# Storing the high part of the experts' gate and up weights by itself, ahead of the low part's subtraction

## The chip, the cores and the metric

The kernel runs on one core of a Trainium2 chip. The metric is the device time of one execution in microseconds (us); lower is better. The numbers of before are the median of 3 runs and one profiled execution.

## What is computed

Two pre-norm layers on 2048 tokens of 512 features, all in float32. The part that matters here is the first attention and the weights that are prepared beside it:

```python
x = x + _L0_attn_ref(_layernorm(x), Wq, bq, Wk, bk, Wv, bv, Wo, bo)   # 2 sequences of 1024 tokens, 16 heads of 32
x = x + _L0_ffn_ref(_layernorm(x), gate_w, w_gate_proj, w_up_proj, w_down_proj)   # 32 experts, 8 of them for each token
x = x + _L1_attn_ref(_layernorm(x), w_in, w_param, w_out)             # state-space layer
x = x + _L1_ffn_ref(_layernorm(x), lut, gate_idx, up_idx, down_idx)   # weights from a 16-entry table

# _L0_ffn_ref, what an expert e computes
g = jnp.einsum('th,eih->tei', x, w_gate_proj)     # i = 192 columns
u = jnp.einsum('th,eih->tei', x, w_up_proj)
h = jax.nn.silu(g) * u * masked_w[:, :, None]
out = jnp.einsum('tei,ehi->th', h, w_down_proj)
```

## The kernel before

The kernel is written by hand, engine by engine. Each stage is a block in which every engine has its own instruction list and semaphores order them; the next block begins when all engines have ended this one. The stages are: layernorm and q, k, v projection; attention (`attend`); output projection; mixture of experts; state-space layer; table feed-forward.

Products in float32 precision are made as sums of three products of a rounded "high" part (type fp32r) and the "low" rest. The experts' weights are split into those two parts before the mixture of experts needs them, on GpSimd (POOL), beside the attention, and are stored in a DRAM tensor `w_split`, from which the mixture of experts reads them for every block of tokens.

In `attend` there are 16 heads, two to a loop body, the first and the last body written out and six turns of a loop between them. POOL's list for one head, in the order of the code, is:

- `take_v` (L577): it copies the head's values into `v_pair`, one of two buffers, which TensorE (PE) needs for the head's outputs (L752, `ps_y<-probs,v_pair`). TensorE waits on `v_ready` for it, `take_v` waits until the head before the last has been used up.
- twice (for two experts) `split_gate_up` (L581 to L596): a cast of `e_raw_gu` (128 partitions x 1536 elements, 6 KB each) into the first half of `e_gu_parts` (L588), a subtraction into the second half (L591), one transfer of both halves to `w_split`, 12 KB of each partition (L594), and the load of the expert after next into `e_raw_gu` (L567). Ahead of the cast it waits for the load, and for the store of the head before out of the same of two buffers (`gu_stored`).
- after each of them `split_down` (L598 to L619): two casts (L607, L608), two subtractions (L611, L614), the store of `e_dn_parts` (L617), of which there is one buffer, and the next load (L570). Ahead of L607 it waits until the store of the expert before has landed (`dn_stored`).

After the 32 experts POOL splits the output projection's weights (L637, L640) and ends its list with waits for all stores. All transfers issued by POOL use queue q0, those issued by SyncE (SP) use q1. SP loads the next heads' q and k (L651, L655) and stores the head's output rows out of `y_st` (L667, L668), for which DVE's copy L860 of the next head waits. The next block, `output_projection`, begins with the load `o_sums<-prob_sums` (L925).

Of the kernel before, what the change touches and what calls it, by code (L numbers as in the profile page):

```python
# [6 lines left out]
F32 = mybir.dt.float32  # L7
# [19 lines left out]
HEADS = 16  # L27
# [463 lines left out]
def attend(nc, qk, v_rows, yT, all_sums, w_raw, w_split, wo, wo_hi, wo_lo):  # L491
# [18 lines left out]
    GU, DN = W_GU, W_RAW - W_GU  # L510
# [3 lines left out]
    with ExitStack() as ctx:  # L514
# [11 lines left out]
        gu_parts, dn_parts = [sb(f"e_gu_parts{x}", [P, 2 * GU], F32R) for x in range(2)], sb("e_dn_parts", [P, 3 * D], F32R)  # L526
# [9 lines left out]
        gu_stored, dn_stored = [sem(f"e_gu_stored{x}") for x in range(2)], sem("e_dn_stored")  # L536
# [8 lines left out]
        def _(pool):  # L545
# [20 lines left out]
            def load_gu(p, x):  # L566
                pool.dma_start(raw_gu[x][:, :], w_raw[bass.ds(p, 1), :, :GU].rearrange("e p c -> p (e c)")).then_inc(gu_loaded[x], 16)  # L567
# [11 lines left out]
            def split_gate_up(it, e, x, final):  # L579
                u = unit(it, e)  # L580
                p = u * 2 + x  # L581
                hi = gu_parts[x][:, :GU]
                pool.wait_ge(gu_loaded[x], u * 16 + 16)
                pool.sem_inc(turns_begun, 1)
                if not start(it, e):
                    pool.wait_ge(gu_stored[x], u * 16)
                    pool.sem_inc(turns_begun, 1)
                nc.gpsimd.tensor_copy(hi, raw_gu[x][:, :]).then_inc(gu_split, 1)  # L588
                pool.wait_ge(gu_split, p * 2 + 1)
                pool.sem_inc(turns_begun, 1)  # L590
                nc.gpsimd.tensor_tensor(gu_parts[x][:, GU:], raw_gu[x][:, :], hi.bitcast(F32), ALU.subtract).then_inc(gu_split, 1)  # L591
                pool.wait_ge(gu_split, p * 2 + 2)
                pool.sem_inc(turns_begun, 1)
                pool.dma_start(w_split[bass.ds(p, 1), :, :2 * GU].rearrange("e p c -> p (e c)"), gu_parts[x][:, :].bitcast(F32)).then_inc(gu_stored[x], 16)  # L594
                if not final:
                    load_gu(p + 2, x)  # L596

# [23 lines left out]
            def body(it, final):  # L621
                for e in range(E):
                    take_v(it, e)
                    for x in range(2):
                        split_gate_up(it, e, x, final and e == E - 1)
                        split_down(it, e, x, final and e == E - 1)
# [12 lines left out]
            pool.sem_inc(turns_begun, 1)  # L639
            nc.gpsimd.tensor_tensor(wo_lo[:, :, :], raw_wo[:, :, :], wo_hi[:, :, :].bitcast(F32), ALU.subtract).then_inc(wo_split, 1)  # L640
            for x in range(2):
                pool.wait_ge(gu_stored[x], 16 * HEADS)
            pool.wait_ge(dn_stored, 16 * EXPERTS)

        @block.sync
# [143 lines left out]
        def _(act):  # L789
# [9 lines left out]
            def body(it, final):  # L799
                act.wait_ge(warmed, it + 1)  # L800
                nc.scalar.activation(warm[:, :], ident[:, 0:1], ACT.Exp).then_inc(warmed, 1)
                for e in range(E):
                    for j, (_, _, width) in enumerate(CHUNKS):
                        for a in range(BATCH):
                            n = unit(it, e) * PER_UNIT + j * BATCH + a
                            act.wait_ge(pv_done, n + 1)
                            act.wait_ge(cols_done, n + 1)
                            nc.scalar.activation(probs[a][j % RING][:, :width], ps_c[(j * BATCH + a) % BUFS][:, :width], ACT.Exp, scale=SCALE).then_inc(exp_done, 1)  # L808
                        if j == 2:
                            shift(it, e, 1)  # L810
                        if j == 8 and not (final and e == E - 1):
                            shift(*after(it, e), 0)
# [1971 lines left out]
```

## Time and profile before

| what | us |
|---|---|
| median of 3 runs (2588.51 to 2600.49) | 2592.28 |
| the profiled execution's own time | 2587.39 |
| its span, first to last instruction | 2585.9 |
| attention with the experts' split, POOL's first expert to the next block's first load | 190 to 634 |

In the views of the trace, times are us from the span's start. "Busy" is time in which an engine executed; "idle before" is how long the engine stood still just before an instruction or a group, and behind the arrow stands what ended it. PEclk is TensorE's granted clock as a share of full speed, DMA the mean busy share of the core's 16 DMA engines.

### The profile page before, as it was taken

The page shows a single profiled execution, that of the slowest core. Times are in us where ns is not written, and L with a number is a line of the kernel's source. Part 1 is how long each engine was busy: PE and PEld are TensorE (multiplying, and loading weights), DVE is VectorE, ACT ScalarE, POOL GpSimd, SP SyncE. Part 2 cuts the span into 40 slices and gives each one's busy share as a digit, 9 for nine tenths or more (in the row PEclk, how much of TensorE's full clock was granted, in tenths as well). Part 3 has the DMA queues.
Part 4 walks back from the last instruction along what each step waited for, and adds up shares of the span by engine and source line. Part 5 has one row for each costly group of instructions (what it writes and reads, how often), then busy time and mean ns, then how long its engine had stood idle before and what let it go on. Part 6 is the DMA issues. An engine that isn't in the chain of part 4 may idle for free. (4 is left out here: it accounts for less than half of the span.)

```text
span 2585.9 us, 48018 instructions
## 1 busy us (share of the span) xinstructions
PE 2338.6 (90%) x12710; PEld 1780.5 (69%) x12712; DVE 1505.8 (58%) x3155; ACT 979.0 (38%) x2202; POOL 1093.8 (42%) x993
## 2 busy tenths in 40 slices
PE   7969898996756999999999779999989998899998
PEld 5855454453635888988888648888856665788886
DVE  6436666663566555555555356999346665655554
ACT  3114555553254444444444342222255554311111
POOL 3128888776003665666667411111256663000000
PEclk9978999998866999999999879999999999999999
DMA  5458999996355999999999644446589761000001
GB/s 177 125 164 314 341 332 335 341 326 252 117 200 163 266 278 278 254 257 271 262 256 214 114 140 137 171 170 216 162 209 219 167 171 30 20 25 24 24 10 66
DMA packets 263308, 491.20 MB, mean 190 GB/s; under 512 B 31889, under 2 KB 149137, under 8 KB 253458
## 3 DMA queue, kind: packets, MB, share of 16 engines
q1 hardware_dynamic: 197202, 272.17, 34.3%
q0 software_dynamic: 62976, 212.42, 29.1%
q10 hardware_dynamic: 3024, 5.29, 0.6%
q8 instruction: 55, 0.90, 0.1%
q14 instruction: 51, 0.42, 0.1%
HBM read 592.96 MB, written 198.79 MB: 306 GB/s over the span
## 5 line engine op out<-in xcount | busy, mean ns | idle before, releaser
L1433 PE MATMUL m_ps_u<-m_ring,m_xT_hi 128*128 x1280 | 369.8, 350 | 0.5 <-DVE m_xT_lo L1543 0.5
L1399 POOL DMA_INDIRECT expert_sum<-x_res,token_of x160 | 256.2, 1601 | 189.4 <-DMA expert_sum<-x_res,token_of 71.1
L808 ACT ACTIVATE probs<-ps_c 128x512 f32<-128x512 f32 (+3 forms) x384 | 179.7, 491 | 208.3 <-PE ps_c L741 105.4
L1433 PEld LDWEIGHTS m_ps_u<-m_ring,m_xT_hi 128*128 128x128 f32 x1280 | 235.9, 189 | 1.2 <-issue 0.9
L709 PE MATMUL ps_r<-k_st,q_st 96*128 96x512 f32 (+3 forms) x384 | 164.6, 435 | 57.8 <-DVEq L831 22.3
L1433 PE MATMUL m_ps_u<-m_ring,m_xT_lo 128*128 x640 | 216.5, 338 | 0.0
L1392 POOL DMA_INDIRECT m_xg<-x_rows,token_of x160 | 172.6, 1078 | 100.6 <-issue 92.6
L1871 PE MATMUL s_ps<-s_x_hi,s_w_hi 128*128 128x512 f32 x512 | 199.7, 390 | 1.6 <-POOL s_w_lo L1841 1.6
L1871 PE MATMUL s_ps<-s_x_lo,s_w_hi 128*128 128x512 f32 x512 | 199.2, 389 | 0.0
L1871 PE MATMUL s_ps<-s_x_hi,s_w_lo 128*128 128x512 f32 x512 | 199.2, 389 | 0.0
L2638 DVE TENSOR_TENSOR x_res<-f_ps_o,x_res 128x512 f32<-128x512 f32 x176 | 109.3, 684 | 142.8 <-PE f_ps_o L2531 142.8
L1557 DVE SCALAR_TENSOR_TENSOR m_h<-m_silu,m_xg,m_ps_u 128x128 f32<-128x128 f32 x160 | 55.6, 348 | 233.3 <-ACT m_silu L1496 233.3
L1453 PE MATMUL m_ps_y<-m_ring,m_hT_hi 128*128 x480 | 178.1, 425 | 9.8 <-issue 8.3
L838 DVE TENSOR_REDUCE neg_max<-ps_r 128x1 f32<-128x512 f32 (+3 forms) x256 | 138.1, 584 | 62.0 <-PE ps_r L711 31.7
L1919 ACT ACTIVATE s_out<-s_ps 128x512 f32<-128x512 f32 x128 | 76.5, 599 | 254.0 <-PE s_ps L1871 254.0
L739 PE MATMUL ps_c<-q_st,k_st 128*128 128x512 f32 (+3 forms) x384 | 162.6, 428 | 0.6 <-ACT probs L808 0.5
L1839 POOL CAST s_w_hi<-s_raw 128x512 fp32r<-128x512 f32 x32 | 23.2, 726 | 308.7 <-PE s_ps L1871 215.5
L752 PE MATMUL ps_y<-probs,v_pair 128*33 128x512 f32 (+3 forms) x768 | 152.3, 521 | 0.0
L1496 ACT ACTIVATE m_silu<-m_ps_u 128x192 f32<-128x192 f32 x160 | 53.0, 331 | 235.9 <-PE m_ps_u L1433 235.9
L1502 ACT COPY x_res<-m_ps_y 128x512 f32<-128x512 f32 x160 | 94.1, 588 | 113.8 <-PE m_ps_y L1453 113.8
L709 PEld LDWEIGHTS ps_r<-k_st,q_st 96*128 96x128 f32 x384 | 83.2, 217 | 73.2 <-issue 22.9
L2251 PE MATMUL s_ps_o<-s_w_out_sb,gated 128*128 128x512 f32 x256 | 125.1, 615 | 5.7 <-DVE gated L2378 3.9
(357 smaller groups left out, 5793.7 us busy)
## 6 DMA issues: line engine op xcount, KB each, us to landing
m_ring<-w_split SPq DMA_DIRECT2D x160, 1536.0 KB
m_ring<-w_split SPq DMA_DIRECT2D x160, 768.0 KB
w_split<-e_gu_parts POOLq DMA_DIRECT2D x32, 1536.0 KB
proj<-s_out SPq DMA_DIRECT2D x32, 1024.0 KB, 3.9
e_raw_gu<-w_experts POOLq DMA_DIRECT2D x32, 768.0 KB
w_split<-e_dn_parts POOLq DMA_DIRECT2D x32, 768.0 KB
e_raw_dn<-w_experts POOLq DMA_DIRECT2D x32, 512.0 KB
q_st<-q_parts SPq DMA_DIRECT2D x32, 256.0 KB
```

Of the source, the lines that this page charges most:

```text
L709: last = nc.tensor.matmul(ps[:, :w], q_st[e][:K_QK, a, tb * P:(tb + 1) * P], k_st[e][:K_QK, a, c:c + w], start=True, stop=not diagonal)
L739: last = nc.tensor.matmul(ps[:, :width], k_st[e][:, a, s * P:(s + 1) * P], q_st[e][:, a, t0:t0 + width], start=True, stop=not diagonal)
L752: nc.tensor.matmul(ps_y[a * COL:a * COL + VW, t0 % HALF:t0 % HALF + width], v_pair[e][:, a * TB + s, :], probs[a][j % RING][:, :width], st ...
L808: nc.scalar.activation(probs[a][j % RING][:, :width], ps_c[(j * BATCH + a) % BUFS][:, :width], ACT.Exp, scale=SCALE).then_inc(exp_done, 1)
L838: nc.vector.tensor_reduce(dst, ps_r[n % BUFS][:, :w], AX.X, ALU.max, negate=True).then_inc(max_done, 1)
L1392: pool.indirect_dma_start(xg[j % X_TURNS][:, :], None, x_rows, rows_at(j), bounds_check=PADDED - 1, oob_is_err=True).then_inc(x_loaded[j % ...
L1399: pool.indirect_dma_start(acc[j % 2], rows_at(j), y[j % TURNS], None, bounds_check=PADDED - 1, oob_is_err=True, compute_op=ALU.add).then_i ...
L1433: last = nc.tensor.matmul(ps_u[b % 2][:, :W_UP], x[b % 2][:, k, :], ring[:, first + k * GU_ROW:][:, bass.ds(place, W_UP)], start=(n == 0), ...
L1453: last = nc.tensor.matmul(ps_y[b % 2][:, :], a[b % 2][:, c, :], ring[:, first:][:, bass.ds(place, D)], start=(n == 0), stop=(n == len(term ...
L1871: last = nc.tensor.matmul(ps[g][:, :], w[:, k, :], x[:, k, of_group(g)], start=(n == 0), stop=(n == 3 * KD - 1))
L2251: last = nc.tensor.matmul(ps_o[tt][:, :], gated[b][:, k, tt * P:(tt + 1) * P], w_o[:, k, :], start=(k == 0), stop=(k == KO - 1))
L2638: nc.vector.tensor_tensor(x_res[:, i, :], ps_o[s][:, :], x_res[:, i, :], ALU.add).then_inc(added, 1)
```

## The change

Per expert, the one 12 KB transfer becomes two of 6 KB rows. The first, of the high half, stands between the cast and the subtraction, behind the wait for the cast that stood there already; the second, of the low half, stands where the one transfer stood. The semaphore `gu_stored` counts two transfers per expert, so its waits count 32 instead of 16.

```diff
                 if not start(it, e):
-                    pool.wait_ge(gu_stored[x], u * 16)
+                    pool.wait_ge(gu_stored[x], u * 32)
                     pool.sem_inc(turns_begun, 1)
                 nc.gpsimd.tensor_copy(hi, raw_gu[x][:, :]).then_inc(gu_split, 1)
                 pool.wait_ge(gu_split, p * 2 + 1)
                 pool.sem_inc(turns_begun, 1)
+                pool.dma_start(w_split[bass.ds(p, 1), :, :GU].rearrange("e p c -> p (e c)"), hi.bitcast(F32)).then_inc(gu_stored[x], 16)
                 nc.gpsimd.tensor_tensor(gu_parts[x][:, GU:], raw_gu[x][:, :], hi.bitcast(F32), ALU.subtract).then_inc(gu_split, 1)
                 pool.wait_ge(gu_split, p * 2 + 2)
                 pool.sem_inc(turns_begun, 1)
-                pool.dma_start(w_split[bass.ds(p, 1), :, :2 * GU].rearrange("e p c -> p (e c)"), gu_parts[x][:, :].bitcast(F32)).then_inc(gu_stored[x], 16)
+                pool.dma_start(w_split[bass.ds(p, 1), :, GU:2 * GU].rearrange("e p c -> p (e c)"), gu_parts[x][:, GU:].bitcast(F32)).then_inc(gu_stored[x], 16)
                 if not final:
                     load_gu(p + 2, x)
...
             for x in range(2):
-                pool.wait_ge(gu_stored[x], 16 * HEADS)
+                pool.wait_ge(gu_stored[x], 32 * HEADS)
```

The added line moves all line numbers behind L590 by one. In POOL's instruction list of the loop, one expert's gate and up weights stand like this before (a row is a line, an operation, the tile written and the tiles read; ISA and REGISTER_ALU are semaphore, address and register instructions):

```order
L588 CAST e_gu_parts<-e_raw_gu 128x1536
L589 ISA
L591 TENSOR_TENSOR e_gu_parts<-e_raw_gu,e_gu_parts 128x1536
L592 REGISTER_ALU
L594 ISA
L594 DMA w_split<-e_gu_parts 128x3072
L567 ISA
L567 DMA e_raw_gu<-w_experts 128x1536
L605 REGISTER_ALU
L607 CAST e_dn_parts<-e_raw_dn 128x512
```

One transfer of 3072 elements a partition follows the subtraction. In the changed kernel the same stretch of POOL's list is:

```order
L588 CAST e_gu_parts<-e_raw_gu 128x1536
L589 ISA
L591 ISA
L591 DMA w_split<-e_gu_parts 128x1536
L592 TENSOR_TENSOR e_gu_parts<-e_raw_gu,e_gu_parts 128x1536
L593 REGISTER_ALU
L595 ISA
L595 DMA w_split<-e_gu_parts 128x1536
L567 ISA
L567 DMA e_raw_gu<-w_experts 128x1536
L606 REGISTER_ALU
L608 CAST e_dn_parts<-e_raw_dn 128x512
```

A transfer and its address instruction have come between the cast and the subtraction; nothing else has moved.

## Rows read from the trace of the kernel before

**Rows 1.** The stage by --windows: us, busy (x instructions) per engine, clock, DMA, GB/s
```profile
190.00:624.00 434.00, 396.88 (x2143) 216.62 (x2143) 270.53 (x485) 223.06 (x461) 352.11 (x331) 0.93 0.92 331
250.00:600.00 350.00, 318.14 (x1759) 174.22 (x1758) 224.60 (x402) 181.30 (x375) 282.47 (x269) 0.95 0.94 336
```
**Rows 2.** POOL's waits, 190 to 624 us: total us, times, longest
```profile
POOL w_split L617 <- POOL e_dn_parts L614: 23.4, 32, 0.8
POOL w_split L594 <- POOL e_gu_parts L591: 23.4, 32, 0.8
POOL e_dn_parts L607 <- DMA w_split<-e_dn_parts: 8.8, 12, 1.3
...
POOL e_gu_parts L591 <- POOL e_gu_parts L588: 5.9, 32, 0.2
...
POOL e_gu_parts L588 <- DMA e_raw_gu<-w_experts: 4.5, 1, 4.5
```
**Rows 3.** POOL in order of time, one expert: start, duration, instruction, idle before
```profile
300.15 3.46 POOL L591 TENSOR_TENSOR e_gu_parts<-e_raw_gu,e_gu_parts 128x1536 fp32r<-128x1536 f32 x1 [0.18 <-POOL e_gu_parts L588]
304.38 0.56 POOL L594 DMA_DIRECT2D w_split<-e_gu_parts  x1 [0.77 <-POOL e_gu_parts L591]
304.99 0.55 POOL L567 DMA_DIRECT2D e_raw_gu<-w_experts  x1
305.53 0.62 POOL L607 CAST e_dn_parts<-e_raw_dn 128x512 fp32r<-128x512 f32 x1
306.08 0.62 POOL L608 CAST e_dn_parts<-e_raw_dn 128x512 fp32r<-128x512 f32 x1
...
310.42 0.56 POOL L617 DMA_DIRECT2D w_split<-e_dn_parts  x1 [0.78 <-POOL e_dn_parts L614]
311.03 0.55 POOL L570 DMA_DIRECT2D e_raw_dn<-w_experts  x1
311.62 1.46 POOL L588 CAST e_gu_parts<-e_raw_gu 128x1536 fp32r<-128x1536 f32 x1
```
**Rows 4.** The same engine, first expert to last and the end of its list
```profile
191.93 1.47 POOL L588 CAST e_gu_parts<-e_raw_gu 128x1536 fp32r<-128x1536 f32 x1 [4.51 <-DMA e_raw_gu<-w_experts]
...
624.30 1.88 POOL L637 CAST wo_hi<-raw_wo 128x2048 fp32r<-128x2048 f32 x1
626.37 4.49 POOL L640 TENSOR_TENSOR wo_lo<-raw_wo,wo_hi 128x2048 fp32r<-128x2048 f32 x1 [0.18 <-POOL wo_hi L637]
```
**Rows 5.** DVE and SP's queue at the end of attention and the next block's start
```profile
626.61 0.69 DVE L860 COPY y_st<-ps_y 128x512 f32<-128x512 f32 x1 [10.89 <-PE ps_y L752]
...
628.43 0.28 SPq L668 DMA_DIRECT2D prob_sums<-y_st  x1
633.62 0.37 SPq L925 DMA_DIRECT2D o_sums<-prob_sums  x1
...
635.74 1.75 DVE L980 RECIPROCAL o_sums<-o_sums 128x256 f32<-128x256 f32 x1 [8.44 <-DMA o_sums<-prob_sums]
```
**Rows 6.** POOL's copy of the values for heads 2 and 15 (of 16, first is 0)
```profile
244.08 0.61 POOL L577 COPY v_pair<-v_rows 128x512 f32 x1
...
600.62 0.61 POOL L577 COPY v_pair<-v_rows 128x512 f32<-128x512 f32 x1
```
**Rows 7.** TensorE's first output products of heads 2 and 15
```profile
259.38 1.70 PE L752 MATMUL ps_y<-probs,v_pair 128*33 128x512 f32 x8
...
611.22 1.70 PE L752 MATMUL ps_y<-probs,v_pair 128*33 128x512 f32 x8
```
**Rows 8.** Waits of TensorE and DVE for transfers, 190 to 624 us: total us, times, longest
```profile
PE ps_r L709 <- DMA q_st<-q_parts: 21.9, 11, 3.0
...
DVE y_st L860 <- DMA prob_sums<-y_st: 21.5, 14, 3.6
```
**Rows 9.** The page: busy time, the packets, queue q0, and the transfers concerned
```profile
PE 2338.6 (90%) x12710; PEld 1780.5 (69%) x12712; DVE 1505.8 (58%) x3155; ACT 979.0 (38%) x2202; POOL 1093.8 (42%) x993
...
DMA packets 263308, 491.20 MB, mean 190 GB/s; under 512 B 31889, under 2 KB 149137, under 8 KB 253458
...
q0 software_dynamic: 62976, 212.42, 29.1%
...
w_split<-e_gu_parts POOLq DMA_DIRECT2D x32, 1536.0 KB
...
e_raw_gu<-w_experts POOLq DMA_DIRECT2D x32, 768.0 KB
w_split<-e_dn_parts POOLq DMA_DIRECT2D x32, 768.0 KB
```
**Rows 10.** POOL's transfer issues by --lines, 190 to 624 us: busy us, mean ns, idle before
```profile
L594 POOL DMA_DIRECT2D w_split<-e_gu_parts x32 | 17.9, 558 | 23.4 <-POOL e_gu_parts L591 23.4
...
L567 POOL DMA_DIRECT2D e_raw_gu<-w_experts x30 | 16.4, 545 | 4.0 <-issue 2.6
```

## The prediction

> **What bounds the kernel now.** I read the stage windows first. The change touches only the stretch from 190 to 624 us, in which POOL splits the experts beside the attention. There TensorE is busy 397 of 434 us, POOL 352, and the DMA engines 92%, 94% in the steady part [rows 1]. Three resources are near their limit, so shares don't tell which of them sets the end.
>
> The waits tell it. POOL's idle time is almost all of its own making: behind each big instruction it waits for that instruction to complete, 0.18 us ahead of an arithmetic one and 0.73 us on average (23.4 / 32) ahead of a transfer [rows 2]. For something outside, it waited 8.8 us in 12 pieces for the down weights' store and 4.5 us once for the first load [rows 2]. No row has POOL waiting for the attention. So POOL's list is one chain of 32 equal pieces: it runs from 191.93 to 624.30 us, 13.5 us an expert, then 6.56 us for the output weights, to 630.86 [rows 4].
>
> What ends the stage? The attention's last copy is at 626.61 and its last store is issued by 628.71; the next block's first load starts at 633.62 [rows 5]. From the start of that load of 128 KB to its first use takes 2.12 us [rows 5], so I take as much for the attention's last store, whose issue begins at 628.43: it has landed by about 630.5. POOL ends at 630.86. The two finish together, POOL by a hair the later, and some 2.8 us of block change follow. **POOL has no slack at the end**: what lengthens its chain lengthens the kernel. The stages behind start as late as the stage ends and work on the same data, so I carry the shift to the end one for one.
>
> **The change, part by part.** Per expert:
>
> 1. An issue is added. The row for an issue with 6 KB rows is the raw load's: 545 ns; the store of 12 KB rows took 558 [rows 10]. The length of a row does not show in it, so the second store is no cheaper than the old one and the first costs about 0.56. 32 x 0.56 = 17.9 us.
> 2. The wait ahead of that issue. Before, the subtraction stood behind the cast with 0.18 us between them. Now a transfer stands there, and transfers behind an arithmetic instruction start 0.73 us after its end on average, 0.77 in the loop, at both places where the trace has one [rows 2, 3]. The trace has no transfer directly behind a cast; its nearest rows are these two, and the subtraction's own gap of 0.18, if nothing in the 0.77 belonged to the transfer. I take the transfers' gap, because it comes behind the completion of the instruction ahead, with semaphore and address instructions to run first, and these are added here as well. 32 x (0.73 - 0.18) = 17.6 us; by the other bound 0.
> 3. The subtraction then stands behind an issue whose completion it need not wait for. The row for that is the cast L607 behind L567, at 0.54 after the issue's start [rows 3]: no gap. Nothing is added.
> 4. The second store stands where the old one stood, with the same gap: nothing.
> 5. What it gives back: the down weights' store of the expert before must land ahead of L607, and POOL waited at most 1.3 us for it, 8.8 in all [rows 2]. L607 now comes 0.56 + 0.55 = 1.11 us later, the high half has left some 4 us earlier, and the same bytes are spread over a longer period. I take all of the 8.8 us as gone; the other end is none.
> 6. The wait on `gu_stored` is for transfers of the head before, two experts and 27 us back. It has no row in the waits; both halves together are the same bytes, so nothing.
>
> Sum: 17.9 + 17.6 - 8.8 = **+26.7 us**. Its lower bound is 17.9 - 8.8 = +9.1, the upper one 17.9 + 17.6 = +35.5.
>
> **Who waits behind POOL.** `take_v` is in POOL's list, so TensorE's values come later, head by head: 2 x 1.11 = 2.2 us less what is given back. At head 2 the values are ready 14.7 us before their first use (244.08 + 0.61 to 259.38), at head 15 still 10.0 us (600.62 + 0.61 to 611.22) [rows 6, 7]. The lag at head 15 would be 15 x 2.2 - 8.3 = 25 us. So somewhere behind the seventh head TensorE begins to wait for POOL, and head 15's values come at about 626. From its first output to the last copy took 16.1 us (611.22 to 627.30) [rows 5, 7], so the attention would end near 642, while POOL ends at 630.86 + 26.7 = 657.6. Between them lie 15 us: enough to cover a slower clock of a TensorE that waits, and a reason not to add TensorE's wait to POOL's.
>
> What is relieved is then worth nothing. TensorE waited 21.9 us for q and DVE 21.5 us for the stores of the output rows [rows 8]. A store in shorter rows, and a DMA load of the same bytes over 461 instead of 434 us (share 0.92 x 434 / 461 = 0.87), should make these waits shorter, but the attention's end lies 15 us ahead of POOL's.
> Here the Trainium skill has a rule in favour of the change: on the page "DMA: Bandwidth & Descriptors", section Queues, rings and completion order, an engine takes turns between queues only at a packet's end, so shorter packets of q0 would let SP's through sooner. The waits for q agree that SP's loads stand behind other transfers, but no row tells by how much a shorter packet would help.
>
> It has one against the change as well. The same page, section Bandwidth, says to make transfers of at least 1 MiB, and its fit gives a transfer some 2.0 us apart from its bytes. By the page that would be an estimated 64 us more for 32 more transfers if none overlapped. The trace has transfers of 768 KB in the same queue beside those of 1536 KB [rows 9] at a busy share of 0.94 [rows 1], which speaks for overlap, and the sum above leaves this out.
>
> **The rivals.**
>
> *The DMA engines become the bound, or the given-back wait stays.* For: a share of 0.94. Their packets took 0.92 x 434 = 399 us; the engines would bind only above the new 461 us, that is if packets took 15% longer, while 4096 packets more are 1.6% of 263308 [rows 9]. A weaker form is likelier: the store's landing keeps pace with POOL and the 8.8 us are waited for as before. That gives 2592.3 + 35.5 = 2628. Chance 0.12.
>
> *Only the issue counts.* If the first store starts 0.18 us behind the cast, as the subtraction did, the sum is +9.1: 2601, within the 0.5%. Against it stand 64 gaps ahead of stores, 46.8 us in all [rows 2], none of them this short on average. Chance 0.07.
>
> *The issue runs beside the subtraction.* Writing the descriptors might not hold back arithmetic that needs nothing of it; then nothing is added and the 8.8 us of waits for the down store go, because the high half has left the queue sooner. POOL ends at 622, the attention with shorter waits a little ahead of 627, and the kernel takes up to 8.8 us less: 2584. This decides if POOL's path grows by less than 8.8 / 32 = 0.28 us an expert. Against it: L607 needs nothing of the load L567 and yet starts only when its issue is over, and so for L588 behind L570 [rows 3]. Chance 0.05, of which 0.02 for more than 13 us.
>
> *The change does not do what it says.* If the first store did not leave ahead of the subtraction there would be one more issue and no relief. POOL's list has it ahead, so what is left of this is the weaker form above.
>
> **How the numbers follow.** The forecast, POOL's chain longer by 26.7 us, has 0.76. The profiled execution took 2587.4 us, its sum is 2614.1; the median of the three runs is 4.9 us higher at 2592.3, and from it the forecast is **2619 us**. Measurement of this kernel can tell about 0.5%, 13 us. The range goes from 2606, half way between the forecast and the case of the issue alone, to 2632, which takes in the upper bound and the scatter of the runs (2588.5 to 2600.5). Slower than by 13 us are the forecast and the first rival: 0.88. Within 0.5%: 0.10, from the issue alone and most of the third rival. Faster: 0.02.
>
> **What the changed profile would show.** The high store's issue L591 with 32 of 0.56 us and an idle time before it of 23 us (the rival: 6); L592 with no idle time before it; POOL busy 1094 + 18 = 1112 us with 1025 instructions; 4096 packets more; the wait ahead of L608 (was L607) near 0; the last expert done at about 651 and `wo_lo` ended at 657 to 658, the load L926 of `o_sums` at 660; TensorE or its weight load waiting for `v_pair` of the late heads; the DMA share near 0.87. I am wrong if L592 starts before L591's issue is over, if L591 starts 0.2 us behind the cast, if new waits for `w_split` stand on POOL, or if the next block starts before 645.

## The result and the profile after

| | before | the change |
|---|---|---|
| median of the runs | 2590.41 (4 runs, 2588.51 to 2600.49) | 2623.26 (4 runs, 2619.68 to 2628.84) |
| ratio | | 1.0111, 95% interval 1.0094 to 1.0128 |
| profiled execution | 2587.39, span 2585.9 | 2622.58, span 2621.0 |
| POOL's last instruction of the attention block ends | 630.86 | 656.88 |
| the attention's last copy ends | 627.30 | 642.90 |
| next block's first load | 633.62 | 662.41 |

By the medians the change makes the kernel 33 us slower (by the ratio's interval 24 to 33); 2619 was forecast, in a range of 2606 to 2632. First the waits of POOL in the changed kernel, 190 to 660 us (what was waited for; us in total, times, longest), the answer to [rows 2]:

```profile
POOL w_split L591 <- POOL e_gu_parts L588: 22.5, 32, 0.8
POOL w_split L618 <- POOL e_dn_parts L615: 22.5, 32, 0.8
POOL w_split L595 <- POOL e_gu_parts L592: 22.5, 32, 0.7
...
POOL e_gu_parts L588 <- DMA e_raw_gu<-w_experts: 5.0, 1, 5.0
```

There is a third group of gaps, as long as the two that were there, and the wait for the down store is no longer in the list. The same stretch by groups (busy us, mean ns of one | idle before), the answer to [rows 10]:

```profile
L592 POOL TENSOR_TENSOR e_gu_parts<-e_raw_gu,e_gu_parts 128x1536 fp32r<-128x1536 f32 x32 | 111.0, 3468 | 0.5
...
L608 POOL CAST e_dn_parts<-e_raw_dn 128x512 fp32r<-128x512 f32 x32 | 19.9, 623 | 0.0
...
L591 POOL DMA_DIRECT2D w_split<-e_gu_parts x32 | 17.0, 533 | 22.5 <-POOL e_gu_parts L588 22.5
```

The added issue is busy 17.0 us and has 22.5 us of idle time before it; the subtraction behind it has nearly none left (5.9 before). One expert in order of time, to be laid beside [rows 3]:

```profile
304.59 1.47 POOL L588 CAST e_gu_parts<-e_raw_gu 128x1536 fp32r<-128x1536 f32 x1
306.80 0.53 POOL L591 DMA_DIRECT2D w_split<-e_gu_parts  x1 [0.74 <-POOL e_gu_parts L588]
307.35 3.49 POOL L592 TENSOR_TENSOR e_gu_parts<-e_raw_gu,e_gu_parts 128x1536 fp32r<-128x1536 f32 x1
311.57 0.55 POOL L595 DMA_DIRECT2D w_split<-e_gu_parts  x1 [0.73 <-POOL e_gu_parts L592]
```

Cast to subtraction is 2.76 us where it was about 1.65. The end of the stage, the answer to [rows 4, 5]:

```profile
642.21 0.69 DVE L861 COPY y_st<-ps_y 128x512 f32<-128x512 f32 x1 [10.90 <-PE ps_y L753]
...
652.39 4.49 POOL L641 TENSOR_TENSOR wo_lo<-raw_wo,wo_hi 128x2048 fp32r<-128x2048 f32 x1 [0.18 <-POOL wo_hi L638]
662.41 0.37 SPq L926 DMA_DIRECT2D o_sums<-prob_sums  x1
```

The attention is over 14 us before POOL, and the block ends with POOL. And the waits of TensorE and DVE (the vector engine), beside [rows 8]:

```profile
PE ps_y L753 <- POOL v_pair L577: 30.0, 11, 4.1
...
DVE y_st L861 <- DMA prob_sums<-y_st: 3.0, 2, 1.9
...
PE ps_r L710 <- DMA q_st<-q_parts: 0.6, 1, 0.6
```

TensorE waits for POOL now, 30 us in 11 pieces (its weight loads 6 more), and hardly at all for q. Part of that is real relief and part is not. Up to 330 us, before the attention's first wait for POOL, TensorE with its weight loads waited 1.5 us for q where before had 7.2, and DVE 3.0 us for the stores where before had 8.3. Behind that the attention stands waiting for POOL at each head, and its loads arrive meanwhile. So the transfers did get somewhat out of the attention's way (DMA share 0.89 from 190 to 651 us), but in the kernel's time nothing came of it.

### The profile page after: what moved, and what is told of

The parts are those of the page before. It is cut to its first block and busy times, and to the rows that moved or that the text cites. A ratio compares the mean times of both kernels' runs of the same rounds, so it can differ in the third digit from the quotient of the medians.

```text
span 2621.0 us, 48098 instructions
## 1 busy us (share of the span) xinstructions
PE 2344.7 (89%) x12710; PEld 1779.3 (68%) x12712; DVE 1490.9 (57%) x3155; ACT 976.9 (37%) x2202; POOL 1113.5 (42%) x1025
## 2 busy tenths in 40 slices
DMA packets 267916, 491.20 MB, mean 187 GB/s; under 512 B 32401, under 2 KB 149649, under 8 KB 262162
## 5 line engine op out<-in xcount | busy, mean ns | idle before, releaser
L753 PE MATMUL ps_y<-probs,v_pair 128*33 128x512 f32 (+3 forms) x768 | 162.2, 547 | 30.3 <-POOL v_pair L577 30.0
L1454 PE MATMUL m_ps_y<-m_ring,m_hT_lo 128*128 x320 | 126.5, 395 | 0.0
```

What stands on the lines that cost most here:

```text
L753: nc.tensor.matmul(ps_y[a * COL:a * COL + VW, t0 % HALF:t0 % HALF + width], v_pair[e][:, a * TB + s, :], probs[a][j % RING][:, :width], st ...
L1454: last = nc.tensor.matmul(ps_y[b % 2][:, :], a[b % 2][:, c, :], ring[:, first:][:, bass.ds(place, D)], start=(n == 0), stop=(n == len(term ...
```

## The experiments

In all of them "before" is the kernel before, run on the same chip. Differences between profiles are against the one profile of before. The "stage's end" is the issue of the next block's first load, 633.62 in before. The letters of the theories are those of the expectations, which were written down before each run.

**Two stores, both late.** The high store stands right ahead of the low one, behind the subtraction.

```diff
-                pool.dma_start(w_split[bass.ds(p, 1), :, :GU].rearrange("e p c -> p (e c)"), hi.bitcast(F32)).then_inc(gu_stored[x], 16)
                 nc.gpsimd.tensor_tensor(gu_parts[x][:, GU:], raw_gu[x][:, :], hi.bitcast(F32), ALU.subtract).then_inc(gu_split, 1)
...
+                pool.dma_start(w_split[bass.ds(p, 1), :, :GU].rearrange("e p c -> p (e c)"), hi.bitcast(F32)).then_inc(gu_stored[x], 16)
                 pool.dma_start(w_split[bass.ds(p, 1), :, GU:2 * GU].rearrange("e p c -> p (e c)"), gu_parts[x][:, GU:].bitcast(F32)).then_inc(gu_stored[x], 16)
```

> Both halves are stored in 6 KB rows, but one right behind the other after the subtraction: the second transfer of the change without its place. Theory P (POOL's chain sets the stage's end, and an added transfer costs its issue and, only if it stands behind an arithmetic instruction, a gap of its own): POOL gains 32 issues of 0.56 us = 17.8 us and no gap, and gives back some 6 to 9 of the 8.8 us it waited for the down store: 9 to 12 us over before, that is 2600 to 2603, with the attention's last copy well ahead of POOL's end. Rival D (the time went into more and smaller transfers on the DMA engines): the same 64 stores in 6 KB rows cost the same 33 us as in the change, 2623.

2601.92 against 2585.67, ratio 1.0061 (1.0045 to 1.0078), 16 us. POOL's waits:

```profile
POOL w_split L594 <- POOL e_gu_parts L591: 22.6, 32, 0.8
POOL w_split L618 <- POOL e_dn_parts L615: 22.6, 32, 0.8
...
POOL e_dn_parts L608 <- DMA w_split<-e_dn_parts: 0.4, 1, 0.4
```

Two groups of gaps, not three, and 8.4 of the 8.8 us given back. POOL's last instruction ends at 640.88, 10.0 us later: 18.6 for the added issues and the 1.0 us ahead of them, less the 8.4. The same number of 6 KB transfers as in the change, without the gap, costs POOL 10 us instead of 26. Theory D, that the transfers themselves cost the time, is out. The stage ends 12.8 us later, 2.8 more than POOL; the change has that surplus too, and it is taken up below.

**High half in two, and in three.** In the change, the high half goes in two transfers of 3 KB rows, as in the diff, or in three of 2 KB, with `GU // 3`.

```diff
-                pool.dma_start(w_split[bass.ds(p, 1), :, :GU].rearrange("e p c -> p (e c)"), hi.bitcast(F32)).then_inc(gu_stored[x], 16)
+                for c in range(0, GU, GU // 2):
+                    pool.dma_start(w_split[bass.ds(p, 1), :, c:c + GU // 2].rearrange("e p c -> p (e c)"), gu_parts[x][:, c:c + GU // 2].bitcast(F32)).then_inc(gu_stored[x], 16)
```

> The change, with the high half in two transfers of 3 KB rows, one right behind the other: the suspected issue is doubled, the gap is not. Theory P: 32 x 0.55 = 17.6 us more than the change, 2641, and no less, since there are no waits on POOL left to give back. Rival D: 4096 more packets like the change's own, so again as much as the change cost, about 33 us more, 2656. Rival T (TensorE's waits for the values, 36 us, set the end): the same order as P, but POOL's last instruction would not be what the next block follows.

> The change with the high half in three transfers of 2 KB rows, right behind each other: a third point on the line of the issue's cost. Theory P: POOL's last instruction ends 2 x 32 x 0.54 = 35 us behind that of the change, near 692; the run with two high transfers had 17.4. It also asks what sets POOL's final drain, which lasted 1.9 us past POOL's last instruction with 128 transfers in the stage, 4.6 with 160, 7.3 with 192, but 7.9 with the 96 of the run with one store. Theory N (it grows with the transfers issued): 10 us here with 224. Theory W (it is what stands in the descriptor ring since its last wrap, which would fit all four numbers with a wrap each 102 transfers): 1 to 2 us.

In two: 2640.82 against 2585.67, ratio 1.0215 (1.0192 to 1.0237). In three: 2655.53 (2 runs) against 2591.03, ratio 1.0255 (1.0231 to 1.0280). POOL's last instruction of the block starts, in two and in three:

```profile
669.74 4.49 POOL L642 TENSOR_TENSOR wo_lo<-raw_wo,wo_hi 128x2048 fp32r<-128x2048 f32 x1 [0.18 <-POOL wo_hi L639]
```
```profile
690.64 4.49 POOL L642 TENSOR_TENSOR wo_lo<-raw_wo,wo_hi 128x2048 fp32r<-128x2048 f32 x1 [0.19 <-POOL wo_hi L639]
```

That is 17.4 us behind the change for 32 issues without a gap (17.6 expected) and 38.3 us for 64 (35 expected; with three pieces POOL has 6 us of waits marked "issue", with two 4.9, in the change 4.0). With no wait left to give back, an issue costs its full 0.54 us, and rows of 3 or 2 KB instead of 6 add nothing to it.

**Less work on POOL, with one store and with the split store.** Both kernels leave out the subtraction on 64 partitions for the down weights' rest, L614 of before, so that their low parts there are wrong; the first is otherwise the kernel before, the second the change.

```diff
...
-                nc.gpsimd.tensor_tensor(rest[REST_E:, :], raw_dn[x][REST_E:, D:], rest[REST_E:, :].bitcast(F32), ALU.subtract).then_inc(dn_split, 1)
...
```

> The kernel before, without the subtraction on 64 partitions for the down weights' rest (L614), so that w_split holds wrong low parts there: POOL has 32 x (1.27 + 0.18) = 46 us less to do. Theory P with the tie at 630.9 and 630.5 us: the stage's end passes to the attention, so nearly nothing is gained, 0 to 10 us (2581 to 2591), unless the transfers that now come closer together slow the attention. If POOL alone had set the end with the attention well ahead, up to 46 us would be gained, 2545.

> The change, without that same subtraction. POOL has 46 us less to do than in the change and would end at 657 - 46 = 611 us, ahead of the attention. Theory P: the cost of the two stores is then hidden: the time is that of the run without the subtraction and with one store, 2581 to 2591, within 0.5%, and lower than it by what the shorter rows and the earlier high half are worth to TensorE's and DVE's waits (43 us in all before), if they are worth anything. Rival D: the 33 us of the change are still there, 2615.

One store: 2580.19, ratio 0.9970 (0.9951 to 0.9989). Split store: 2578.90, ratio 0.9975 (0.9952 to 0.9997). These are the decisive pair. Of 46 us less on POOL the kernel gets 5.5 (2580.19 against 2585.67): the tie of before is real, and the attention stands right behind POOL. And with POOL at 606 us, off the path, the split store costs nothing that shows: about 30 us with POOL as the bound, and without it the median is even 1.3 us lower. How near to nothing is known only to some 6 us, since the ten executions of each kernel scatter over 21 us (2563.5 to 2584.9 and 2570.3 to 2590.6), and in the two profiles the split store's stage ended 6.7 us later (629.79 against 623.07). It gains nothing that shows either, although TensorE's waits for q fall; in the first and in the second kernel:

```profile
PE ps_r L706 <- DMA q_st<-q_parts: 16.8, 10, 3.2
```
```profile
PE ps_r L707 <- DMA q_st<-q_parts: 4.7, 6, 1.3
```

In the second, TensorE's same products wait more for DVE instead (27.8 us against 12.5). Which of the halves' two properties (leaving early, shorter rows) relieves q is not shown. With both stores late, in short rows, TensorE and its weight loads waited 15.4 us for q, with 12 KB rows behind the casts 11.2, and with nothing but idle instructions added 15.5, all against 25.0 in before: this wait moves by 10 us for other reasons too.

**One store, one store and one load, low part with the down parts.** The opposite of the change: all parts of an expert in one tile (two of these) and one transfer at the expert's end, the loads behind it; then the two loads merged too; and last the high half early, as in the change, with everything else in one transfer at the end.

```diff
+        w_parts = [sb(f"e_w_parts{x}", [P, W_EXPERT], F32R) for x in range(2)]
...
-                pool.dma_start(w_split[bass.ds(p, 1), :, :2 * GU].rearrange("e p c -> p (e c)"), gu_parts[x][:, :].bitcast(F32)).then_inc(gu_stored[x], 16)
-                if not final:
-                    load_gu(p + 2, x)
...
-                pool.dma_start(w_split[bass.ds(p, 1), :, 2 * GU:].rearrange("e p c -> p (e c)"), dn_parts[:, :].bitcast(F32)).then_inc(dn_stored, 16)
+                pool.wait_ge(gu_split, p * 2 + 2)
+                pool.dma_start(w_split[bass.ds(p, 1), :, :].rearrange("e p c -> p (e c)"), w_parts[x][:, :].bitcast(F32)).then_inc(gu_stored[x], 16)
                 if not final:
+                    load_gu(p + 2, x)
                     load_dn(p + 2, x)
```

> The opposite of the change, in the kernel before: one store per expert of all parts, gate, up and down, in 18 KB rows, at the expert's end, and both loads right behind it. POOL loses 32 issues and 32 gaps (32 x 1.11 = 35 us) and its waits for the down store (9 us). Theory P: POOL ends near 587 and the attention sets the end, as in the run with less work on POOL and one store: 2575 to 2585, 3 to 10 us faster than before and far from the 44 us that POOL loses. Rival D: fewer and larger transfers help the DMA engines, and the gain is 20 us or more. Rival Q: longer rows hold up the loads of q (TensorE waited 21.9 us for them in before, 17 to 19 in the run with less work on POOL), these waits grow by 10 us and eat the gain.

> The run with one store, with one load per expert as well, of 8 KB or more per partition: half the transfers of before. In the run with one store POOL waited 48 us for the attention, the attention ended 17 us later than in before, and TensorE waited 34 us for q (25 in before). Theory B (three transfers issued in a burst, or longer rows, hold up the attention's loads): still 8 to 20 us slower than before, with TensorE's waits for q at 30 us or more. Rival M (the new place of the buffers in memory or another accident of that run): near before. The final drain by theory W about 5 us, by N under 1.

> The high half leaves behind its cast in 6 KB rows as in the change, but the low half goes with the down weights' parts in one transfer of 12 KB rows at the expert's end, the loads behind it: as many transfers as in before. POOL's list: one gap of 0.55 us more at the cast, one of 0.73 less at the low half, and no wait for the down store: 32 x 0.18 + 8.8 = 15 us less than before, end near 616. Theory P: the attention sets the end again, 2575 to 2590, within 0.5% of before, that is 33 to 45 us below the change although the high half leaves as early. Rival E (the early transfer itself is what costs): near the change, 2610 or more.

| | ratio, 95% interval | us over before, of the medians | attention's last copy starts | POOL waits for the attention |
|---|---|---|---|---|
| one store | 1.0041 (1.0023 to 1.0058) | +10 | 643.27 | 47.9 |
| one store, one load | 1.0047 (1.0029 to 1.0066) | +7 | 632.22 | 45.8 |
| high first, rest in one | 1.0085 (1.0057 to 1.0113) | +19 | 649.35 | 22.8 |

My expectation for the first and the third was wrong: I gave POOL a shorter list, had it, and the attention became slower than it had been. The rows of the first kernel:

```profile
POOL v_pair L578 <- PE ps_y L746: 47.9, 13, 5.9
PE ps_r L703 <- DMA q_st<-q_parts: 27.3, 13, 5.0
...
PEld ps_r L703 <- DMA q_st<-q_parts: 7.2, 2, 5.3
...
PE ps_r L703 <- DMA k_st<-k_parts: 5.8, 5, 1.5
```

POOL waits for TensorE, and TensorE with its weight loads 34.5 us for q, 25 in before, and 6.2 us for k, for which before has no wait (the two engines overlap, so such a sum is an upper bound). Together these waits are 15.7 us longer, and the attention's last copy comes 16.7 us later. In the other two kernels the numbers do not match as well: with one load the waits for q and k are 15.3 us longer (27.6 and 12.7 us) and the copy 5.6 us later, and with the high half first they are only 6.6 us longer (27.2 and 4.4 us) and the copy 22.7 us later. That this last kernel sends its high half early and still is the slowest of the three shows that leaving early is no gain in itself. Its 2614.95 us is even the number of rival E (2610 or more), by which the early transfer itself costs; against E as a rule stands the pair with less work on POOL, where the early transfer cost nothing that shows.

**The store behind the casts, and a second down buffer.** In the kernel before, L594 and the load behind it are put behind the casts L607 and L608. The second kernel has besides the tiles of the one-store kernels, so that the down parts have two buffers.

```diff
...
                 nc.gpsimd.tensor_copy(rest, raw_dn[x][:, D:]).then_inc(dn_split, 1)
                 nc.gpsimd.tensor_copy(hi, raw_dn[x][:, :D]).then_inc(dn_split, 1)
+                pool.wait_ge(gu_split, p * 2 + 2)
+                pool.sem_inc(turns_begun, 1)
+                pool.dma_start(w_split[bass.ds(p, 1), :, :2 * GU].rearrange("e p c -> p (e c)"), gu_parts[x][:, :].bitcast(F32)).then_inc(gu_stored[x], 16)
+                if not final:
+                    load_gu(p + 2, x)
```

> The kernel before, with the store of gate and up and the load behind it moved behind the two casts for the down weights, so that the subtraction it must wait for has long ended when its turn comes. It asks what the gap ahead of a transfer is, 0.70 to 0.73 us against 0.18 ahead of arithmetic, half of what the change added. Theory G (the gap comes with the transfer, whatever arithmetic instruction stands ahead of it): the gap is again 0.7 and POOL's list gets no shorter, 2590 within 0.5%. Theory H (the gap is the wait for the subtraction's completion plus the instructions behind that wait): it falls to 0.2 or less, POOL's list is up to 32 x 0.55 = 17 us shorter, the attention sets the end, and the kernel is 3 to 8 us faster than before, like the run with less work on POOL and one store.

> The kernel before with the store behind the casts, as in the run of that name, and a second buffer for the down parts, in one tile with the gate and up parts, the tile that the two runs with one store and the run with the low and down parts together had. POOL waited 37 us for the one down buffer there; here it needn't, and its list is 23 us shorter than in before. It asks why the attention ended late in those three runs (632 to 649 us against 627). Theory B (transfers issued in a burst at the expert's end): the transfers here go out as in before, so the attention ends at 618 to 627 and the time is 0 to 8 us below before. Theory A (the place of the buffers in memory): the attention ends at 635 or later and the time is 5 us or more above before. Rival R (transfers that POOL issues sooner crowd the attention's, whatever their form): also late, and with POOL waiting for the attention 30 us or more.

The gap is gone. POOL's groups in the first kernel:

```profile
L602 POOL CAST e_dn_parts<-e_raw_dn 128x512 fp32r<-128x512 f32 x32 | 19.4, 608 | 37.5 <-DMA w_split<-e_dn_parts 37.3
L617 POOL DMA_DIRECT2D w_split<-e_dn_parts x32 | 17.9, 559 | 23.4 <-POOL e_dn_parts L614 23.4
L606 POOL DMA_DIRECT2D w_split<-e_gu_parts x32 | 17.9, 558 | 0.0
```

The store that has just waited for its subtraction has 23.4 us before it, the one whose subtraction ended two casts ago 0.0. So the 0.73 us does not come with every transfer: it is the wait for the completion and what stands between wait and issue. But the casts now come 0.73 + 0.56 + 0.55 us earlier, and the wait for the one down buffer grew from 8.8 to 37.3 us. POOL ended only 6.6 us earlier, not 17 as theory H had it, and the time is the same instead of 3 to 8 us less: 2587.46 against 2591.03, ratio 0.9991 (0.9973 to 1.0010).

With the second buffer that wait is gone too; POOL ends at 595.7 and the attention sets the end:

```profile
591.23 4.51 POOL L638 TENSOR_TENSOR wo_lo<-raw_wo,wo_hi 128x2048 fp32r<-128x2048 f32 x1 [0.18 <-POOL wo_hi L635]
...
614.88 0.69 DVE L857 COPY y_st<-ps_y 128x512 f32<-128x512 f32 x1 [10.89 <-PE ps_y L749]
```

2585.48 against 2594.31, ratio 0.9960 (0.9943 to 0.9977): 9 us faster than before, the best kernel that leaves nothing out. The stage's end is 14.3 us earlier. Against the three kernels above it has the same tiles but sends four transfers an expert spread out, so theory A (their place in memory) is out, and R too (its DMA share is higher, 0.97 from 190 to 600 us against 0.93 to 0.94, and POOL waits only 9.8 us for the attention). That leaves theory B, which forecast this run nearly right. But B names two things, the burst at the expert's end and longer rows, and they were not told apart: the one with a single load has fewer issues in its burst and yet a slow attention, and the slowest one has no row longer than before. Why the attention was slow in those three is therefore argued, not shown.

**Instructions without work, and the change again.**

```diff
                 pool.wait_ge(gu_split, p * 2 + 1)
+                pool.sem_inc(turns_begun, 1)
+                pool.sem_inc(turns_begun, 1)
                 pool.sem_inc(turns_begun, 1)
```

> The kernel before with two more semaphore increments per expert on POOL that nothing waits for; the transfers are those of before. It asks why the next block began 5.5 us after POOL's last instruction in the change and with both stores late, 8.2 us with the high half in two, and 2.8 us in before. Theory C (POOL's code is longer and one more piece of it has to be fetched): 5.5 us here as well, and with some 1 to 2 us for the increments 3 to 5 us over before. Rival S (the added transfers' completion, or what they leave in the queue, holds POOL's last waits): 2.8 us as in before, and 1 to 2 us over it in all.

> The change once more, on the same chip as its neighbours. The first profile had the stage's end 28.8 us later but the kernel's end 35.1 us later; 6 us came in the later stages, 9 in the mixture of experts and some back in the state-space layer. Theory P: POOL ends at 657 +- 1, the next block begins 5.5 us later, and the later stages differ by a few us from one execution to the next: less than 6 us here. Rival L (the stores' new form makes the later stages slower, for instance the mixture of experts reading w_split): again 6 us or more. The time itself: 29 to 33 us over before.

With the idle increments: 2597.80 against 2595.69, ratio 1.0017 (0.9997 to 1.0037), stage's end 2.76 us behind POOL as in before: the number of rival S (2.8), not of theory C (5.5), for increments in these places. The change again: 2623.34 against 2595.69, that is 27.7 us, a little less than the 29 to 33 expected, ratio 1.0110 (1.0074 to 1.0145), POOL's end at 657.69 and the stage's end 5.53 us behind, both as in its first profile. But its later stages were 11.2 us longer than those of before, 6.3 in its first profile. That is Rival L's number. In the other profiles of kernels whose high half isn't stored apart the same difference is 9.9 us (one store), 6.9 (second down buffer), 3.5 (idle increments), 2.4 (one store, one load), 1.9 (less POOL work, one store) and -1.5 (store behind the casts); in the other ones with the high half apart it is 6.2 (in two), 3.4 (in three), 3.2 (both late), 2.4 (rest in one) and 0.2 (less POOL work, split store). So it does not follow the form of the stores; single profiles differ by such amounts behind the attention, and before's was among the short ones. What makes them differ was not looked for.

## Why the prediction was right

**What bounds.** POOL's chain, with no slack: shown by the pair with less work on POOL, from both sides. POOL was forecast to end at 657.6 and ended at 656.88, 26.0 us later against 26.7.

**The terms.** Step 1, the issue: 17.9 forecast, 17.0 measured. Step 2, the gap: 17.6 forecast, 22.5 - (5.9 - 0.5) = 17.1 measured, and its nature (completion, then the instructions up to the issue) shown by the store behind the casts. Step 3, no gap behind an issue: 0.5 us in 32. Step 5, the given-back wait: all of the 8.8. Step 6: no row. The waits that were not touched moved by less than 2 us each way (4.0 us of waits marked "issue" instead of 2.6; 0.9 less at each of the two old gaps). Two figures of the working were wrong, and neither carried weight. Half way between the forecast and the case of the issue alone lies 2610, not the 2606 from which the range goes. And 4608 packets more came, not 4096 (267916 against 263308): 512 of them are under 512 B (32401 against 31889), 16 for each added transfer.

**Who waits behind POOL.** The attention's end was forecast near 642 and its last copy ended at 642.90. TensorE first waited for the values at 334 us, at the sixth head, not behind the seventh: relieved of its waits for q the attention ran ahead of its old pace, which I had named but not carried into that date. The DMA share was 0.89 where I had 0.87.

**What the forecast lacked.** The stage ended 28.8 us later, not 26.7, since 5.5 us instead of 2.8 lie between POOL's last instruction and the next block. I had taken the block change as fixed. The rest to the 33 us of the medians lies in the later stages, within what single executions scatter; measured again, the whole cost was 27.7 us. So 2619 was 4 us low. That it was not 6 us low (26.7 forecast, 32.9 between the medians) is luck: the forecast started from 2592.28, and the fourth run of before brought that median down to 2590.41. The forecast's case was the one that happened.

**The rivals.** The weaker form of the DMA rival (8.8 us waited for as before) is out, as is the issue beside the subtraction: L592 starts when L591's issue is over. "Only the issue counts" was the case of the kernel with both stores late, at +16 us rather than +9. The rule on transfers of at least 1 MiB (the Trainium skill, "DMA: Bandwidth & Descriptors", section Bandwidth), with the fixed 2.0 us a transfer of the fit in the same page's section on the anatomy of one DMA, from which an estimated 64 us came for 32 more, does not show where POOL is not the bound: ratios 0.9970 and 0.9975. The rule of the Trainium skill that a DMA engine changes queues only at a packet's end (same page, section Queues, rings and completion order) fits the waits for q up to 330 us, 7.2 us before and 1.5 after. It is not shown to be the reason, since in kernels with 12 KB rows the wait over the whole stage fell from 25.0 to 11.2 and 15.5 as well, and in the kernel's time nothing of it shows.

## What to carry to other kernels

Splitting a transfer to let one half leave early is paid by the engine that issues it, here 0.53 us each time for the issue and 0.53 for a wait that arithmetic did not need; look whether that engine has slack at the stage's end before asking what the DMA engines would like. Put a store behind work that does not depend on it, not behind the instruction it must wait for, and check which buffer's wait is uncovered then. Where two engines end together, shortening one alone is worth little (5.5 us here for 46 us less work), and a shorter list that sends its transfers in another order can even slow the other.

## What was not expected of the hardware

Between POOL's last instruction and the next block lies a drain of its sequencer. Here it is in before and in the change (count, duration in ns, start):

```profile
L514 POOLq DRAIN  x1: 5236/5236/5236, 627.5 to 627.5; - x1
```
```profile
L514 POOLq DRAIN  x1: 8024/8024/8024, 653.5 to 653.5; - x1
```

It ends at 632.7 and 661.5: 1.9 and 4.6 us past the last arithmetic, beside which it had begun. (In the runs with 64 and 96 transfers it began only behind the arithmetic, and there its whole duration is counted.) Over all runs that remainder goes with the transfers that POOL issued in the block, but not in one direction: 64 transfers 5.3 us, 96 7.9, 128 1.8 to 1.9 (before and five other kernels), 160 4.6 to 4.7 (the change twice and two more), 192 7.3, 224 2.1. Per transfer it rises by some 0.085 us and falls back by 8 to 9 us twice on the way. The last two counts run, 64 and 224, were forecast before they ran (about 5, and 1 to 2) by supposing that the count starts again every 102 transfers, which fitted the first four. That is a guess that has held twice; what the engine does in that time no row shows. The longer drain cost the change 2.8 of its 33 us, and where the attention ends last (4.5 us from its last copy's start to the next block in both kernels with less work on POOL) it is hidden.
